# Four TensorE steps more for a quarter of the keys: merging runs of 128 to 256 in the matmul network of a sort on Trainium2

## The chip, the cores and the metric

The kernel runs on one core of a Trainium2 chip. The metric is the device time of one execution in microseconds (us), where less is better.

## What is computed

The input is 4 images of 64 x 64 tokens with 256 channels. The part that takes the time is the first layer. Each token is normalised over its channels, correlated with all 4,096 tokens of its image, and the 4,096 correlations are sorted; 256 evenly spaced ranks of the sorted row are added to the token:

```python
corr = jnp.einsum('bmf,bnf->bmn', x3, x3) / F
s = -jnp.sort(-corr, axis=-1)
ranks = jnp.round(jnp.linspace(1.0, M - 1, NB_POOLS)).astype(jnp.int32)
pooled = jnp.take(s, ranks, axis=-1)
```

After it comes a mixture of four experts with two layers each (256 to 512 to 256, GELU between), whose weights for a token come from a graph attention over 1,048,576 edges.

## The kernel before

`prepare` and `rank` (to about 4,290 us) normalise the tokens and work out where each edge goes. `pool_rows` is the sorting stage, to about 30,412 us. After it `segment_max`, `segment_sum`, `route` and `combine` do the attention and put the outputs together.

`pool_rows` works on 64 pairs of token tiles (2 x 128 tokens). A token's row of 4,096 keys lies in one partition, the two tiles being two halves `g` of the work. The sort has two parts.

**The front** sorts groups of 128 keys. TensorE and ScalarE do it on data that lie with the keys in the partitions. A comparison of keys a and z is written as a sum and a difference: TensorE multiplies by a matrix that gives a + z and a - z (`net`, built from `group_matrices`), ScalarE takes the absolute value (`ACT.Abs`, line 1189), and the next matrix makes (sum + |difference|) / 2 and (sum - |difference|) / 2 as part of its own sums. One such step is a tick. The 32 groups of a token's keys are handled in 4 rounds (`ROUNDS`) of 2 slots (`s`), each slot with 4 groups in two banks of PSUM. A round before the change has 29 ticks (`TICKS`):

- tick 0, the correlation: 8 matmuls of 256 columns a slot (line 992), copied by line 1186;
- 20 ticks whose comparisons stay within 64 wires (`BLOCK_TICKS`): four matmuls of 64 x 64 with 512 columns a slot, one in each quarter of the array (line 999). The prediction calls them tile ticks;
- 7 ticks of 128 x 128 matmuls, two a slot (line 1003): full ticks;
- the last, which turns the keys back so that tokens lie in the partitions (line 1008), copied by line 1195 into `fresh`.

A slot's next matmuls wait for ScalarE's copy of that slot (`fe_copied`), and ScalarE for them (`fe_ready`), so that one slot's matmuls run beside the other slot's copy. All operands are float32, and the profile counts two matmul records for each matmul.

**The merges** of the sorted runs, from 128 to 4,096, are VectorE's: 50 stages (`STAGES`), each with a pair (p, k), counted 0 to 49 in what follows. Stages 0 to 7 have p = 128, 8 to 16 p = 256, 17 to 26 p = 512, 27 to 37 p = 1,024, 38 to 49 p = 2,048. A stage does a maximum and a minimum (lines 1165 and 1166) for each half `g`. The last four stages (`SPARSE`, line 1141) compare only what the wanted ranks need. In a stage with k < p some keys at the ends of each run of 2p are not compared; ScalarE copies them to the other buffer (`carry`, line 1237): p keys of each 2p when k = p/2, half as many at each further stage.

**The order.** VectorE sorts pair i while TensorE and ScalarE do the front of pair i + 1 and the experts' layers (FFN) of pair i - 1. Nothing is scheduled by a planner. `ticks_of` spreads the ticks of a pair evenly over VectorE's first 48 stages; ScalarE's program (`period`) goes stage by stage: the copy of a stage for g = 0, its share of ticks, the copy for g = 1, more ticks. ScalarE's copy of stage s waits until VectorE has ended stage s - 1 (`sorted_`); VectorE's stage s + 1 waits for the copy of stage s (`carried`). VectorE's stage 0 waits for the whole front of its pair (line 1159). The FFN pieces on TensorE stand between ticks at fixed numbers: for expert e the first layer at ticks 31 + 20 e and the next, GELU on ScalarE at tick 34 + 20 e, the second layer at ticks 37 + 20 e and the next. `residual` follows VectorE's stage 4 and `normalise` stage 8. GpSimd scatters the edges all the while and is waited for by no one in this stage.

Of the kernel before, what the change touches and what calls it, by code (L numbers as in the profile page):

```python
# [16 lines left out]
F32 = mybir.dt.float32  # L17
BF16 = mybir.dt.bfloat16
I32 = mybir.dt.int32
ALU = mybir.AluOpType  # L20
# [3 lines left out]
P = 128  # L24
# [7 lines left out]
BANK = 512  # L32
# [38 lines left out]
C_ALL = C_LIFT + 1  # L71
# [7 lines left out]
def group_stages():  # L79

    out, p = [], 1
# [10 lines left out]
def group_pairs(p, k):  # L92
    out = []
    for at in range(0, WIRES, 2 * p):
        if k == 0:
            out += [(at + n, at + 2 * p - 1 - n) for n in range(p)]
        else:
            out += [(c + n, c + k + n) for c in range(at, at + 2 * p, 2 * k) for n in range(k)]
    return out


GROUP_STAGES = group_stages()
TICKS = len(GROUP_STAGES) + 1
BLOCK_TICKS = [t for t, (p, k) in enumerate(GROUP_STAGES) if t > 0 and 2 * p <= HALF]
assert len(BLOCK_TICKS) % 2 == 0


def group_matrices():

    out, wires = [], None
    for p, k in GROUP_STAGES:
        block = HALF if 2 * p <= HALF else WIRES
        rows = [(m // (block // 2) * block + m % (block // 2), pair) for m, pair in enumerate(group_pairs(p, k))]
        if wires is None:
            wires = np.eye(WIRES, dtype=np.float32)
        stage = np.zeros((WIRES, WIRES), np.float32)
        for r, (a, z) in rows:
            stage[:, r] = wires[:, a] + wires[:, z]  # L120
            stage[:, r + block // 2] = wires[:, a] - wires[:, z]
        out.append(stage)
        wires = np.zeros((WIRES, WIRES), np.float32)
        for r, (a, z) in rows:
            wires[r, a] = wires[r + block // 2, a] = wires[r, z] = 0.5
            wires[r + block // 2, z] = -0.5
    return out + [wires]


C_TOTAL = C_NET + TICKS * WIRES  # L130


def shape_constants():
# [14 lines left out]
    c[:, C_NET:] = np.concatenate(group_matrices(), 1)  # L148
# [20 lines left out]
N_FULL = N_STAGES - SPARSE  # L169

# [77 lines left out]
def build(nc, x, w_gat, att_src, att_dst, b_gat, ln_gamma, ln_beta, w1, b1, w2, b2, edges, consts, out):  # L248
# [35 lines left out]
    net = sb("net", [P, TICKS, WIRES], F32)  # L284
# [55 lines left out]
def prepare(nc, b):  # L340
# [50 lines left out]
    with nc.Block() as block:  # L391
        @block.sync
        def _(sp):

            sp.dma_start(b.cst[:], b.consts[:, 0:C_ALL]).then_inc(const_in, 16)
            sp.dma_start(b.net[:].rearrange("p t w -> p (t w)"), b.consts[:, C_NET:]).then_inc(const_in, 16)
# [1436 lines left out]
```

## Time and profile before

Three runs took 33,436.27 to 33,437.55 us, median 33,436.87. The profiled execution took 33,442.64 us, and the span of its profile is 33,441.0 us.

| engine | busy us | share of the span |
|---|---|---|
| TensorE, matmuls (PE) | 26,912.7 | 80% |
| TensorE, weight loads (PEld, beside PE) | 12,865.6 | 38% |
| VectorE (DVE) | 29,959.0 | 90% |
| ScalarE (ACT) | 20,929.2 | 63% |
| GpSimd (POOL) | 16,416.8 | 49% |

| group | count | busy us |
|---|---|---|
| tile ticks, matmul records, line 999 | 81,920 | 10,881.2 |
| full ticks, matmul records, line 1003 | 14,336 | 6,422.3 |
| copies with absolute value, line 1189 | 13,824 | 13,748.3 |
| maxima of the merges, line 1165 | 5,888 | 12,122.0 |
| minima of the merges, line 1166 | 5,888 | 12,114.5 |
| copies of kept keys, line 1237 | 5,632 | 3,338.5 |

Busy time of PE is modelled, so a busy PE is not PE at its peak. A duration is longer than the distance to the next start on the same engine, since the end of one instruction overlaps the beginning of the next; for sums, starts are compared. In a row of the timeline, square brackets give the idle time ahead of the instruction and what ended it. "issue" means that the engine waited for nothing that the profile shows.

### The profile page before, as it was taken

Reading aid. Unit: us, or ns where it says so; the run is one execution under the profiler, and the core shown is the slowest. Engines: PE = TensorE matmul, PEld = TensorE weight load, DVE = VectorE, ACT = ScalarE, POOL = GpSimd, SP = SyncE. Lnnn points to the kernel's source line nnn. Section 1 sums busy time; section 2 is a strip of 40 time slices with the busy share of each in tenths; the row PEclk is TensorE's granted clock in tenths of the full one; section 3 lists DMA queues with packets and bytes.
Section 4 is the critical chain, followed back from the end, with each engine's and each line's share of the span. In section 5 each row is a group of like instructions: output and inputs, shape, how many; then the busy total and the mean of one; then the engine's idle time right before and its main releaser. Section 6 shows DMA issues by size and latency. Waiting matters only on the chain. (4 is left out here: it accounts for less than half of the span.)

```text
span 33441.0 us, 482974 instructions
## 1 busy us (share of the span) xinstructions
PE 26912.7 (80%) x157939; PEld 12865.6 (38%) x158452; DVE 29959.0 (90%) x32518; ACT 20929.2 (63%) x31151; POOL 16416.8 (49%) x9076
## 2 busy tenths in 40 slices
PE   3888888888888888888888888888888888873464
PEld 3555533333333333333333333333333333332364
DVE  6888859999999999999999999999999999997744
ACT  2777766666667676667666666766766766760010
POOL 0000038888888888888888888883000000003520
PEclk8999999999999999999999999999999999996655
DMA  2000000000000000000000000000000000000103
GB/s 85 2 2 2 2 17 6 6 7 6 6 6 11 6 7 6 7 6 7 6 11 7 6 6 6 7 6 6 10 6 5 6 6 5 6 5 12 12 11 126
DMA packets 651133, 394.32 MB, mean 12 GB/s; under 512 B 424844, under 2 KB 604048, under 8 KB 646160
## 3 DMA queue, kind: packets, MB, share of 16 engines
q1 hardware_dynamic: 337746, 311.61, 3.0%
q0 software_dynamic: 290304, 22.40, 1.0%
q8 instruction: 1430, 23.43, 0.3%
q10 hardware_dynamic: 20288, 25.70, 0.2%
q14 instruction: 1365, 11.18, 0.1%
HBM read 196.68 MB, written 162.34 MB: 11 GB/s over the span
## 5 line engine op out<-in xcount | busy, mean ns | idle before, releaser
L1189 ACT ACTIVATE z<-psum 128x1024 f32<-128x1024 f32 x13824 | 13748.3, 1027 | 4795.4 <-PE psum L1003 2380.5
L1301 POOL DMA_INDIRECT sorted_d<-word_s,place_s x8192 | 15441.3, 1885 | 2646.8 <-issue 2476.9
L999 PE MATMUL psum<-z,net 64*64 64x512 f32 x81920 | 10881.2, 632 | 2974.8 <-ACT z L1189 2877.8
L1165 DVE TENSOR_TENSOR arena<-arena 128x2048 f32<-128x2048 f32 (+9 forms) x5888 | 12122.0, 2059 | 1216.7 <-ACT arena L1237 729.1
L1166 DVE TENSOR_TENSOR arena<-arena 128x2048 f32<-128x2048 f32 (+9 forms) x5888 | 12114.5, 2057 | 0.0
L1003 PE MATMUL psum<-z,net 128*128 128x512 f32 x14336 | 6422.3, 602 | 366.9 <-ACT z L1189 365.6
L999 PEld LDWEIGHTS psum<-z,net 64*64 64x64 f32 x81920 | 2567.8, 135 | 10337.6 <-issue 10323.0
L1452 POOL DMA_INDIRECT arena<-table_d,arena x752 | 901.6, 1199 | 8210.3 <-issue 7724.9
L1237 ACT ACTIVATE arena<-arena 128x2048 f32<-128x2048 f32 (+8 forms) x5632 | 3338.5, 594 | 1384.6 <-DVE arena L1166 1139.7
L1003 PEld LDWEIGHTS psum<-z,net 128*128 128x128 f32 x14336 | 2706.7, 192 | 3821.1 <-issue 2538.8
L823 ACT ACTIVATE arena<-cst,arena 128x128 bf16<-128x128 f32 x8320 | 2633.5, 389 | 608.4 <-PE psum L751 510.8
L1295 POOL DMA_DIRECT2D word_s<-words_d x64 | 37.4, 584 | 4802.1 <-issue 4664.9
L992 PE MATMUL psum<-rows,arena 128*128 128x256 f32 x8192 | 1836.3, 382 | 152.0 <-issue 120.2
L676 DVE TENSOR_SCALAR arena<-iota_bf,arena 128x256 bf16<-128x256 bf16 x8287 | 1791.7, 279 | 5.8 <-PE psum L751 5.7
L992 PEld LDWEIGHTS psum<-rows,arena 128*128 128x128 f32 x8192 | 1542.6, 191 | 379.3 <-issue 151.9
L712 DVE TENSOR_REDUCE arena<-psum 128x512 f32 x2048 | 1410.3, 689 | 289.6 <-PE psum L782 164.3
L1186 ACT ACTIVATE z<-psum,cst 128x1024 f32<-128x1024 f32 x512 | 570.1, 1113 | 1503.6 <-PE psum L992 1503.6
L1436 PE MATMUL psum<-cst,arena 128*128 128x128 f32 x3008 | 651.0, 407 | 972.2 <-DVE arena L1410 972.2
L1048 PE MATMUL psum<-arena,hid 128*128 128x256 f32 x4096 | 1144.5, 403 | 189.8 <-ACT hid L1221 189.8
L740 PE MATMUL psum<-arena,order_bf 128*128 128x128 bf16 x8320 | 851.4, 227 | 495.4 <-DVE arena L676 482.8
L1035 PE MATMUL psum<-tt,arena 128*128 128x256 f32 x4096 | 1131.1, 400 | 4.3 <-ACT tab L1213 4.3
L1141 DVE TENSOR_TENSOR arena<-arena 128x146 f32<-128x146 f32 (+16 forms) x3584 | 1037.5, 378 | 41.0 <-DVE arena L1141 24.1
(213 smaller groups left out, 16717.4 us busy)
## 6 DMA issues: line engine op xcount, KB each, us to landing
sorted_d<-word_s,place_s POOLq DMA_INDIRECT x8192
y_d<-ys SPq DMA_DIRECT2D x256, 256.0 KB
arena<-y_d SPq DMA_DIRECT2D x64, 1024.0 KB, 5.6
arena<-in_x SPq DMA_DIRECT2D x34, 512.0 KB, 5.1
x<-in_x SPq DMA_DIRECT2D x65, 256.0 KB
xnt_d<-arena SPq DMA_DIRECT2D x32, 512.0 KB, 3.1
hk_d<-arena SPq DMA_DIRECT2D x32, 512.0 KB, 4.3
arena<-hk_d SPq DMA_DIRECT2D x4, 4096.0 KB, 14.2
```

The lines of the kernel that those rows point to most:

```text
L676: last = nc.vector.tensor_scalar(hot_pair(slot, j), b.iota_bf[:], tile, None, ALU.is_equal)
L712: nc.vector.tensor_reduce(places[:, bass.ds(k * SUPER + g * 4, 4)], psum[:, g % 4, :].rearrange("p (q c) -> p q c", c=P), AX.X, ALU.max).t ...
L823: last = nc.scalar.activation(steps[:, j % RING, :], b.iota, ACT.Relu, bias=low_s[s][:, j:j + 1], scale=-1.0)
L992: last = nc.tensor.matmul(bank[:, n // 2, n % 2 * 2 * P:(n % 2 + 1) * 2 * P], b.xnt[:, c, key:key + WIRES], rows[:, c, :], start=(c == 0), ...
L999: last = nc.tensor.matmul(psum[n * HALF:(n + 1) * HALF, 2 * s + r, :], b.net[rr, t, rr], flat[rr, n * BANK:(n + 1) * BANK], start=True, st ...
L1003: last = nc.tensor.matmul(bank[:, n, :], b.net[:, t, :], flat[:, n * BANK:(n + 1) * BANK], start=True, stop=True)
L1048: nc.tensor.matmul(psum[:, 6 + g, 0:D], hid[:, m, g * P:(g + 1) * P], b.w2s[:, e, m, :], start=(m == 0), stop=False)
L1165: nc.vector.tensor_tensor(hi_out, hi_in, lo_in, ALU.max)
L1166: nc.vector.tensor_tensor(lo_out, hi_in, lo_in, ALU.min).then_inc(sorted_[g], 1)
L1189: last = nc.scalar.activation(flat, bank, ACT.Abs)
L1237: nc.scalar.activation(carried_over(half[s % 2][g], p, k), carried_over(half[(s - 1) % 2][g], p, k), ACT.Copy).then_inc(carried[g], 1)
L1301: pool.indirect_dma_start(out=b.sorted_d[:, :], out_offset=bass.IndirectOffsetOnAxis(ap=place_s[:, s, j:j + 1], axis=0), in_=word_s[:, s, ...
```

## The change

In the first of the four rounds the front now goes one level further. Its 1,024 keys leave it as 4 sorted runs of 256 instead of 8 of 128. To that end one of the two groups that are to be merged is sorted in the other order: half of the groups get their correlation with the sign changed (scale -1/D instead of 1/D, in two instructions of half the size), the step that makes both meet adds a bias of +2 or -2 (`C_MEET`), and the wires of a comparison then span 256 keys, of which TensorE sees 128 at a time.

VectorE's stages 0 to 7 and ScalarE's copies there leave out those 1,024 keys of each half (`LO`). Stage 8 reads them from `fresh` and the other 3,072 from where stage 7 left them, with two pairs of instructions for each half. ScalarE may therefore write `fresh` again only after stage 8 of the sort in progress (`FRESH_READ`).

The network of all rounds is laid out anew. Sorting 16 keys takes 9 layers instead of 10, so a round has 28 ticks instead of 29 (the correlation, 26 comparisons, the one out). The wires are split into halves by another of their bits at each level, so that comparisons stay within 64 wires of the array. Where the split changes, a new kind of tick stands, "swapped": four matmuls a slot of 64 rows x 128 columns with 512 columns streamed, two of them adding up in each bank (line 1113). The kinds of ticks:

| | correlation | tile | swapped | full | out | ticks |
|---|---|---|---|---|---|---|
| before, each of 4 rounds | 1 | 20 | 0 | 7 | 1 | 29 |
| after, round 0 | 1 | 29 | 2 | 3 | 1 | 36 |
| after, rounds 1 to 3 | 1 | 24 | 2 | 0 | 1 | 28 |

A pair has 120 ticks instead of 116, spread over the same 48 stages. The numbers at which FFN pieces stand are unchanged.

TensorE's program shows the new kinds. This is the first round of pair 2's front from its first tile tick on, up to the next round's correlation, before; names are the tensors written and read, and x is how many matmuls follow each other:

```order
L999 MATMUL psum<-z,net 64x512 x160
L1003 MATMUL psum<-z,net 128x512 x14
L1017 MATMUL psum<-cst,pooled 128x128 x4
L1003 MATMUL psum<-z,net 128x512 x12
L1025 MATMUL psum<-wtab,tt 128x24 x4
L1003 MATMUL psum<-z,net 128x512 x2
L1008 MATMUL psum<-net,z 128x128 x16
L992 MATMUL psum<-rows,arena 128x256 x16
```

And the same place after, up to the round's last full tick (line 1106 is a tile tick, 1113 a swapped one, 1117 a full one, 1099 the correlation):

```order
L1106 MATMUL psum<-z,net 64x512 x152
L1113 MATMUL psum<-z,net 128x512 x8
L1106 MATMUL psum<-z,net 64x512 x28
L1132 MATMUL psum<-cst,pooled 128x128 x4
L1106 MATMUL psum<-z,net 64x512 x4
L1117 MATMUL psum<-z,net 128x512 x4
L1106 MATMUL psum<-z,net 64x512 x8
L1117 MATMUL psum<-z,net 128x512 x2
L1140 MATMUL psum<-wtab,tt 128x24 x4
L1117 MATMUL psum<-z,net 128x512 x2
L1106 MATMUL psum<-z,net 64x512 x24
L1117 MATMUL psum<-z,net 128x512 x2
```

The block of seven full ticks is gone; single full and swapped ticks stand among tile ticks, and every FFN piece (here 1132 and 1140) keeps its tick number but has other neighbours.

VectorE's program around stages 7 and 8 in the loop, before:

```order
L1165 TENSOR_TENSOR arena<-arena 128x16x127
L1166 TENSOR_TENSOR arena<-arena 128x16x127
L1165 TENSOR_TENSOR arena<-arena 128x16x127
L1166 TENSOR_TENSOR arena<-arena 128x16x127
L1165 TENSOR_TENSOR arena<-arena 128x8x256
L1166 TENSOR_TENSOR arena<-arena 128x8x256
L1165 TENSOR_TENSOR arena<-arena 128x8x256
L1166 TENSOR_TENSOR arena<-arena 128x8x256
```

And after:

```order
L1287 TENSOR_TENSOR arena<-arena 128x12x127
L1288 TENSOR_TENSOR arena<-arena 128x12x127
L1287 TENSOR_TENSOR arena<-arena 128x12x127
L1288 TENSOR_TENSOR arena<-arena 128x12x127
L1287 TENSOR_TENSOR arena<-arena 128x2x256
L1288 TENSOR_TENSOR arena<-arena 128x2x256
L1287 TENSOR_TENSOR arena<-arena 128x6x256
L1288 TENSOR_TENSOR arena<-arena 128x6x256
L1287 TENSOR_TENSOR arena<-arena 128x2x256
L1288 TENSOR_TENSOR arena<-arena 128x2x256
L1287 TENSOR_TENSOR arena<-arena 128x6x256
L1288 TENSOR_TENSOR arena<-arena 128x6x256
```

Stage 7 runs over 12 runs instead of 16, and stage 8 is cut in two parts for each half. The diff, cut to its core:

```diff
+SORT16 = (((0, 5), (1, 4), (2, 12), (3, 13), (6, 7), (8, 9), (10, 15), (11, 14)),
...
+def layers():
+
+    out = [[(c + 15 - b, c + 15 - a) for c in range(0, WIRES, 16) for a, b in layer] for layer in SORT16]
+    p = 16
     while p < WIRES:
-        out.append((p, 0))
+        out.append([(c + n, c + 2 * p - 1 - n) for c in range(0, WIRES, 2 * p) for n in range(p)])
         k = p // 2
         while k >= 1:
-            out.append((p, k))
+            out.append(halving(WIRES, k))
             k //= 2
         p *= 2
...
+LAYERS = [[(side + a, side + z) for side in (0, WIRES) for a, z in layer] for layer in layers()]
+UP_TO_32 = len(LAYERS) - 7
+
+SORT_PLAN = ([("corr", LAYERS[0], by_64)] + [("tile", x, by_64) for x in LAYERS[1:UP_TO_32]]
+             + [("swapped", LAYERS[UP_TO_32], by_bit0)] + [("tile", x, by_bit0) for x in LAYERS[UP_TO_32 + 1:-2]])
+LAST_PLAN = [("tile", LAYERS[-2], by_bit0), ("swapped", LAYERS[-1], no_block)]
+MERGE_PLAN = ([("full", LAYERS[-2], by_bit3), ("tile", LAYERS[-1], by_bit3),
+               ("full", halving(256, 128), by_low)] + [("tile", halving(256, k), by_low) for k in (64, 32, 16)]
+              + [("full", halving(256, 8), by_side)] + [("tile", halving(256, k), by_side) for k in (4, 2)]
+              + [("swapped", halving(256, 1), no_block)])
+
...
+MERGED_ROUNDS = 1
+LO = MERGED_ROUNDS * SLOTS * UNIT_GROUPS * WIRES
+ROUNDS = M // WIRES // UNIT_GROUPS // SLOTS
+FRONT = [ticks_of_round(MERGE_PLAN, len(SORT_PLAN) + 1 + len(LAST_PLAN)) if j < MERGED_ROUNDS else
+         ticks_of_round(LAST_PLAN, len(SORT_PLAN) + 1) for j in range(ROUNDS)]
+TICK_OF = [(j, t) for j in range(ROUNDS) for t in range(len(FRONT[j]))]
+PER_PAIR = len(TICK_OF)
+LAST_FIRST = PER_PAIR - len(FRONT[-1]) + 1
...
+    c[:, C_MEET] = np.where(r % HALF < HALF // 2, 2.0, -2.0)
...
+    FRESH_READ = FIRST_MERGE + 1 if LO > 0 else 1
...
-                elif t in BLOCK_TICKS:
+                elif how == "tile":
                     for r in range(2):
                         rr = slice(r * HALF, (r + 1) * HALF)
                         for n in range(2):
-                            last = nc.tensor.matmul(psum[n * HALF:(n + 1) * HALF, 2 * s + r, :], b.net[rr, t, rr],
-                                                    flat[rr, n * BANK:(n + 1) * BANK], start=True, stop=True)
-                elif t < TICKS - 1:
+                            last = nc.tensor.matmul(psum[n * HALF:(n + 1) * HALF, 2 * s + r, :],
+                                                    b.net[rr, at:at + HALF], flat[rr, n * BANK:(n + 1) * BANK],
+                                                    start=True, stop=True)
+                elif how == "swapped":
+                    for r in range(2):
+                        for n in range(2):
+                            nn = slice(n * HALF, (n + 1) * HALF)
+                            last = nc.tensor.matmul(bank[:, n, :], b.net[nn, at + r * WIRES:at + (r + 1) * WIRES],
+                                                    flat[nn, r * BANK:(r + 1) * BANK], start=(r == 0), stop=(r == 1))
+                elif how == "full":
                     for n in range(2):
-                        last = nc.tensor.matmul(bank[:, n, :], b.net[:, t, :], flat[:, n * BANK:(n + 1) * BANK],
+                        last = nc.tensor.matmul(bank[:, n, :], b.net[:, at:at + WIRES], flat[:, n * BANK:(n + 1) * BANK],
                                                 start=True, stop=True)
                 else:
                     for g in range(2):
                         for n in range(UNIT_GROUPS):
-                            last = nc.tensor.matmul(bank[:, g, n * WIRES:(n + 1) * WIRES],
-                                                    z[s][:, n, g * P:(g + 1) * P], b.net[:, t, :],
+                            place = n % 2 * 2 + n // 2 if j < MERGED_ROUNDS else n
...
+            def sources(s, g):
+
+                last = half[(s - 1) % 2][g]
+                if s < FIRST_MERGE:
+                    return [(fresh[g] if s == 0 else last, LO, M)]
+                if s == FIRST_MERGE and LO > 0:
+                    return [(fresh[g], 0, LO), (last, LO, M)]
+                return [(last, 0, M)]
...
-                        nc.vector.tensor_tensor(hi_out, hi_in, lo_in, ALU.max)
-                        nc.vector.tensor_tensor(lo_out, hi_in, lo_in, ALU.min).then_inc(sorted_[g], 1)
+                        for source, from_, to in sources(s, g):
+                            hi_in, lo_in = compared(source[:, from_:to], p, k)
+                            hi_out, lo_out = compared(half[s % 2][g][:, from_:to], p, k)
+                            nc.vector.tensor_tensor(hi_out, hi_in, lo_in, ALU.max)
+                            last = nc.vector.tensor_tensor(lo_out, hi_in, lo_in, ALU.min)
+                        last.then_inc(sorted_[g], 1)
...
+                    if how == "corr" and j < MERGED_ROUNDS:
+                        for n in range(2):
+                            last = nc.scalar.activation(flat[:, n, :], bank[:, n, :], ACT.Abs,
+                                                        bias=b.cst[:, C_LIFT:C_LIFT + 1],
+                                                        scale=(1.0 - 2.0 * n) / D)
...
+                        if tick + 1 == len(FRONT[0]) and s == 0 and not (isinstance(i, int) and i == 0):
                             for g in range(2):
-                                act.wait_ge(sorted_[g], (i - 1) * N_FULL + 1)
+                                act.wait_ge(sorted_[g], (i - 1) * N_FULL + FRESH_READ)
...
+                    elif meet:
+                        last = nc.scalar.activation(flat, bank, ACT.Abs, bias=b.cst[:, C_MEET:C_MEET + 1])
+                    else:
+                        last = nc.scalar.activation(flat, bank, ACT.Abs)
...
-                nc.scalar.activation(carried_over(half[s % 2][g], p, k), carried_over(half[(s - 1) % 2][g], p, k),
-                                     ACT.Copy).then_inc(carried[g], 1)
+                first = LO if s < FIRST_MERGE else 0
+                nc.scalar.activation(carried_over(half[s % 2][g][:, first:M], p, k),
+                                     carried_over(half[(s - 1) % 2][g][:, first:M], p, k), ACT.Copy).then_inc(carried[g], 1)
```

## Rows read from the trace of the kernel before

**Rows 1.** Windows: length; busy us of PE, PEld, DVE, ACT, POOL; PE clock; DMA

```profile
4286.00:4664.00 378.00, 315.69 (x1815) 126.33 (x1813) 18.88 (x25) 235.06 (x240) 0.00 (x0) 0.95 0.10 36
13000.00:22000.00 9000.00, 7783.70 (x42853) 3289.98 (x42852) 8603.52 (x6049) 6280.78 (x7710) 7620.57 (x4143) 0.98 0.03 7
30412.00:33441.00 3029.00, 1473.35 (x6924) 1389.03 (x6924) 1735.15 (x3239) 169.47 (x406) 901.62 (x752) 0.57 0.18 44
```

**Rows 2.** Waits of VectorE, 10000 to 20000 us: total, times, longest

```profile
DVE arena L1165 <- ACT arena L1237: 289.7, 149, 5.1
DVE pooled L1141 <- ACT arena L1237: 70.5, 25, 3.5
DVE arena L1165 <- issue: 52.3, 25, 2.6
```

**Rows 3.** Timeline of VectorE: start us, us, engine, line, instruction, count [idle before]

```profile
15120.26 2.29 DVE L1165 TENSOR_TENSOR arena<-arena 128x2048 f32<-128x2048 f32 x1 [1.93 <-issue]
...
15129.07 1.22 DVE L1165 TENSOR_TENSOR arena<-arena 128x1024 f32<-128x1024 f32 x1
...
15133.62 1.75 DVE L1165 TENSOR_TENSOR arena<-arena 128x1536 f32<-128x1536 f32 x1
...
15331.04 2.29 DVE L1165 TENSOR_TENSOR arena<-arena 128x2040 f32<-128x2040 f32 x1 [5.14 <-ACT arena L1237]
...
20163.93 2.28 DVE L1165 TENSOR_TENSOR arena<-arena 128x2040 f32<-128x2040 f32 x1 [5.14 <-ACT arena L1237]
...
20298.86 2.16 DVE L1165 TENSOR_TENSOR arena<-arena 128x1920 f32<-128x1920 f32 x1 [4.01 <-ACT arena L1237]
```

**Rows 4.** Waits of ScalarE, 10000 to 20000 us

```profile
ACT arena L1237 <- DVE arena L1166: 311.0, 147, 4.3
```

**Rows 5.** Timeline of TensorE while no other work runs (first unit groups)

```profile
4378.31 24.30 PE L1003 MATMUL psum<-z,net 128*128 128x512 f32 x56
4402.44 3.73 PE L1008 MATMUL psum<-net,z 128*128 128x128 f32 x32
4406.01 7.07 PE L992 MATMUL psum<-rows,arena 128*128 128x256 f32 x32
...
4414.38 2.05 PE L999 MATMUL psum<-z,net 64*64 64x512 f32 x16 [0.28 <-ACT z L1186]
4416.70 1.62 PE L999 MATMUL psum<-z,net 64*64 64x512 f32 x12 [0.27 <-ACT z L1189]
```

**Rows 6.** Timeline of ScalarE, ticks with copies of kept keys

```profile
15129.07 1.93 ACT L1189 ACTIVATE z<-psum 128x1024 f32<-128x1024 f32 x2
...
15132.67 1.95 ACT L1189 ACTIVATE z<-psum 128x1024 f32<-128x1024 f32 x2
15134.48 1.09 ACT L1237 ACTIVATE arena<-arena 128x1024 f32<-128x1024 f32 x1
15135.43 1.97 ACT L1189 ACTIVATE z<-psum 128x1024 f32<-128x1024 f32 x2
```

**Rows 7.** Timeline of TensorE, FFN pieces between ticks

```profile
15230.00 1.09 PE L999 MATMUL psum<-z,net 64*64 64x512 f32 x8
15231.02 1.13 PE L1035 MATMUL psum<-tt,arena 128*128 128x256 f32 x4
15232.08 1.09 PE L999 MATMUL psum<-z,net 64*64 64x512 f32 x8
...
15250.03 1.13 PE L1048 MATMUL psum<-arena,hid 128*128 128x256 f32 x4
...
15258.58 1.95 PE L999 MATMUL psum<-z,net 64*64 64x512 f32 x16
...
15292.82 1.03 PE L1035 MATMUL psum<-tt,arena 128*128 128x256 f32 x4
15293.68 1.88 PE L1003 MATMUL psum<-z,net 128*128 128x512 f32 x4
```

**Rows 8.** The page's costliest groups: count | busy us, mean ns | idle before

```profile
L1003 PEld LDWEIGHTS psum<-z,net 128*128 128x128 f32 x14336 | 2706.7, 192 | 3821.1 <-issue 2538.8
```

More of the change, by code:

```diff
@@ L89, in group_stages @@
     return out
-def group_pairs(p, k):
-    out = []
-    for at in range(0, WIRES, 2 * p):
-        if k == 0:
-            out += [(at + n, at + 2 * p - 1 - n) for n in range(p)]
-        else:
[L98 to L127, printed above, removed]
@@ L130, with by_64, by_bit0, by_bit3 @@
-C_TOTAL = C_NET + TICKS * WIRES
+def by_64(w):
+    return w // 64 % 2
+def by_bit0(w):
+    return (w ^ w // 64) % 2
+def by_bit3(w):
+    return w // 8 % 2
+def by_low(w):
+    return w % 2
+def by_side(w):
+    return w // 128
+def no_block(w):
+    return 0
+def items_of(layer):
+    alone = set(range(2 * WIRES)) - {w for pair in layer for w in pair}
+    return [(0, a, z) for a, z in layer] + [(1, w, w) for w in sorted(alone)] + [(2, a, z) for a, z in layer]
+def in_rows(layer, blocks, at):
+    return sorted(m for m in items_of(layer) if all(f(m[1]) == v for f, v in zip(blocks, at)))
@@ new lines, in wire_from, with matrix @@
+def wire_from(layer, wire):
+    for a, z in layer:
+        if wire == a:
+            return {(0, a, z): 0.5, (2, a, z): 0.5}
+        if wire == z:
+            return {(0, a, z): 0.5, (2, a, z): -0.5}
+    return {(1, wire, wire): 1.0}
+def matrix(before, rows, item_list, turned):
+    m = np.zeros((len(rows), len(item_list)), np.float32)
+    index = {item: n for n, item in enumerate(rows)}
+    for n, (kind, a, z) in enumerate(item_list):
+        for wire, sign in ((a, 1.0),) if kind == 1 else ((a, 1.0), (z, 1.0 if kind == 0 else -1.0)):
+            for item, part in wire_from(before, wire).items() if before else {(1, wire, wire): 1.0}.items():
+                m[index[item], n] += sign * part * (-1.0 if wire >= WIRES and turned else 1.0)
+    return m
@@ new lines, with ticks_of_round @@
+SORT_NET, SORTED_16, INSIDE = plan_matrices(SORT_PLAN, None, None)
+LAST_NET = plan_matrices(LAST_PLAN, SORTED_16, INSIDE)[0]
+MERGE_NET = plan_matrices(MERGE_PLAN, SORTED_16, INSIDE)[0]
+WIRES_NET = matrix(LAYERS[-1], in_rows(LAYERS[-1], (no_block, by_side), (0, 0)), [(1, w, w) for w in range(WIRES)],
+                   False)
+NETS = SORT_NET + [WIRES_NET] + LAST_NET + MERGE_NET
+NET_AT = [sum(m.shape[1] for m in NETS[:n]) for n in range(len(NETS) + 1)]
+NET_COLS = NET_AT[-1]
+def ticks_of_round(plan, first):
+    wires = len(SORT_PLAN)
+    at = [NET_AT[n] for n in list(range(wires)) + list(range(first, first + len(plan)))]
+    out = [(how, a, layer == halving(2 * WIRES, WIRES)) for (how, layer, _), a in zip(SORT_PLAN + plan, at)]
+    return out + [("wires", NET_AT[wires], False)]
@@ L169 @@
 N_FULL = N_STAGES - SPARSE
+FIRST_MERGE = sum(p == WIRES for p, _ in STAGES)
 def compared(buf, p, k):
@@ L974, in _, with front @@
         def _(pe):
-            def front(i, j, t, s):
-                if j == 0 and t == 0 and s == 0:
+            def front(i, tick, s):
+                j, t = TICK_OF[tick]
+                how, at, _ = FRONT[j][t]
+                if tick == 0 and s == 0:
                     pe.wait_ge(hk_in, (i // PAIRS_OF_IMAGE + 1) * 16)
                     pe.wait_ge(rows_in, (i + 1) * 16)
-                before = j * TICKS + t
-                if not (isinstance(i, int) and i == 0 and before == 0):
-                    pe.wait_ge(fe_copied[s], i * PER_PAIR + before)
-                    if t in BLOCK_TICKS:
+                if not (isinstance(i, int) and i == 0 and tick == 0):
+                    pe.wait_ge(fe_copied[s], i * PER_PAIR + tick)
+                    if how in ("tile", "swapped"):
                         pe.sem_inc(b.settled[3], 1)
```

89 lines of the change are left out of this document (54 added, 35 removed), and 8 rows, old and new, of the table SORT16.

## The prediction, made before the kernel after was run

> **What bounds the kernel now.** I read the views from coarse to fine. First the windows: between 13,000 and 22,000 us VectorE is busy 95.6% of the time, TensorE 86%, ScalarE 70%, at a mean TensorE clock of 0.98 [rows 1]. That is the sorting stage, 64 pairs of token tiles from about 4,664 to 30,412 us, and the change touches nothing else but the 378 us ahead of it. Then the waits of VectorE: in 10,000 us it waits 289.7 + 70.5 us for ScalarE's copies (line 1237) and 52.3 us at the loop's turn [rows 2]. The timeline gives the length of a pair: the same wait of 5.14 us comes back after 12 pairs, (20163.93 - 15331.04) / 12 = 402.74 us [rows 3]. In 10,000 us there are thus 24.8 pairs, VectorE waits 16.6 us in each and has work of its own for 386. ScalarE in turn waits 311.0 / 24.8 = 12.5 us a pair for a full stage of VectorE [rows 4]. So VectorE sets the pace, with the TensorE-ScalarE chain close behind. Both must get shorter for a full gain.
>
> **What goes on VectorE.** A stage is four instructions, two for each half. Four of 2,048 elements take 15129.07 - 15120.26 = 8.81 us, four of 1,024 take 4.55 us [rows 3]; so an instruction costs 0.069 us + 1.04 ns an element, start to start. The eight stages of p = 128 hold 2048 + 1024 + 1536 + 1792 + 1920 + 1984 + 2016 + 2032 = 14,352 elements an instruction, and a quarter of them goes: 3,588 x 4 x 1.04 ns = 14.9 us. Stage 8 takes its keys from two places, which adds four instructions of 0.069 us: 0.3 us. Net 14.65 us a pair. The elements themselves stay at the same price, since only the outer count in the access pattern falls from 16 to 12.
>
> **What changes on TensorE and ScalarE.** A tick is one step of the small network for both slots. While no other work runs, the rows give: a tile tick (64x64) 2.31 us (4414.38 to 4416.70), a full tick 24.13 / 7 = 3.45, the tick that brings out the keys 3.6, the correlation 7.0 [rows 5]. Before, a round is one correlation, 20 tile ticks, 7 full ones and one out: 80.9 us. After, three rounds have 24 tile ticks, 2 of the new "swapped" kind and no full one: 66.1 us + 2 S. The first round has 29 tile ticks, 3 full, 2 swapped: 87.9 us + 2 S.
>
> S is in no row. Its slot has four matmuls of 64 rows x 128 columns; the two of a pair lie in different halves of the rows and write different banks. The lower bound is a full tick, 3.45 us, if the two run side by side. The upper bound is 6.9 if they don't, and somewhat more if each also pays a change of shape. The nearest row is the tile slot: four matmuls, in both halves of rows and of columns, take 1.02 us, where one full matmul takes 0.86 (two records of 0.431) [rows 5, 7]. So halves do run side by side, and I stay near the low end. Going from one shape to another costs 0.2 us: an FFN piece takes 1.06 us between tile slots (15231.02 to 15232.08) and 0.86 us in a full stretch (15292.82 to 15293.68) [rows 7]. A swapped tick has two such changes, so S = 3.45 + 0.35 = 3.8. By that, the four rounds go from 323.6 to 316.3 us. On the worst end (6.9) they become 341.
>
> The Trainium skill speaks against the change here. Its page TensorE: Matmul & The Clock Gate, section Part 3: Packing small matmuls, says that a weight load overlaps running matmuls only when its row group differs, and in a swapped slot the second pair's weights go into the rows that the first pair is using. By it S would be near 5. This case's rows say otherwise for one shape: 56 full matmul records in a row, all in the same rows and each with a load of 192 ns, take 0.431 us each, no more than their columns need [rows 5, 8]. I keep that result as the second rival.
>
> ScalarE has eight more slot passes of 0.9 us (1.81 us for two, 15132.67 to 15134.48 [rows 6]), 7.2 us. Its copies for p = 128 shrink by a quarter, about 1.6 us. The correlation of the first round is copied in two pieces, some 0.3 us under the longer matmuls. The new bias goes into a full tick, where ScalarE has time.
>
> **Whether the chain still keeps up.** I add up both engines stage by stage. ScalarE may start stage s's copy when VectorE has ended stage s-1, and VectorE's stage s+1 needs that copy. A tile tick costs 2.31, or 1.81 plus the copy if that is more: with a copy of 2,048 it takes 15132.67 - 15129.07 = 3.60, so the copy is 1.80; one of 1,024 is 0.95 [rows 6]. To it come the FFN pieces: 0.92 for each of 16 first-layer pieces, 1.24 for each of 16 second-layer ones. (15250.03 to 15258.58, with the slot after it 9.57 us for four slots and four pieces, less 4 x 1.16 [rows 7].) GELU adds about 1.5 us four times.
>
> For the kernel before, this sum gives waits of 1.6 and 5.0 us at stage 25 (the trace: 1.5 and 5.14), 3.5 us at stage 42 (4.01 or less) [rows 3], 4.7 at the pair's end, and 399.7 us a pair. So it misses 3 us of 402.74, and it finds the right places: each time the 7 full ticks, the one out and the next correlation put ScalarE behind.
>
> For the kernel after, with S = 3.8, stages 0 to 7 end at 49.1 us on VectorE (64.0 before) and ScalarE's ticks for them at 50.5 (61.3). ScalarE may be one stage late, so the early stages just fit. At stage 14 it stands at 95.7 against 100.3, at stage 25 at 185.0 against 188.2, where before it was 198.5 against 211.7. The waits left are 0.9 at stage 17, 1.7 at 31, 1.2 at 41, some tenths elsewhere and 3.9 at the pair's end, which stays since a swapped tick and the one out stand there as full ones did. The pair takes 378.7 us, 21.0 less: 14.65 of work, 6.3 of waits. With S = 3.45 it is 376.6, with S = 5 386.4.
>
> **Sum.** 62 pairs run with both neighbours: 62 x 21.0 = 1,302 us. The first and the last have no such waits and give 14.65 each: 29. The network ahead of the first pair gives 323.6 - 316.3 = 7. Together 1,338 us. The profiled execution took 33,442.64 us (span 33,441.0), 5.8 over the median of 33,436.87, so I subtract from either alike: 32,105 by the profile, 32,100 by the median. This is 4.0% faster.
>
> **Rivals.**
> 1. The waits don't fall or new ones come, since a swapped tick is dearer (S about 5: four exposed loads of 192 ns in a slot, 3.45 + 2 x 0.77). The pair takes 386.4, 13.3 less; 62 x 13.3 + 29 - 2 = 852 us, so 32,585. For it: the early stages have only some us to spare. Against it: the 56 records above.
> 2. The two halves of a swapped tick run one after the other (S = 6.9). The pair takes 399.7, as before: what VectorE saves it waits at stages 17 to 42. Only the ends differ, 29 saved and 18 lost: 33,425, no change. Against it: the tile slot [rows 7].
> 3. Slower: as rival 2, and each of the four matmuls also pays the 0.2 us of a change of shape, 4 x 1.06 a slot, S = 8.5. The sum gives 410.9 a pair; 62 x 11.2 + 30 - 29 = 695 us more, so 34,130. It decides from S = 6.9 on. Only the place, the eight swapped ticks of each pair, could do it.
> 4. All waits for ScalarE vanish but the pair's end: 402.74 - 14.65 - 12 = 376.1, that is 26.65 less a pair; 62 x 26.65 + 29 + 7 = 1,688 us, so 31,755. The sum finds small waits instead, so this is only the floor.
>
> **Chances.** The forecast has 0.72 (with the part toward the floor), rival 1 has 0.18, rival 2 0.04, rival 3 0.05, and 0.01 is left. The range goes from 31,930 (S = 3.45 and a few more us of waits gone) to 32,620, just beyond rival 1. A change of 0.2% is 67 us, about what a measurement of this kernel can tell from none. Faster is the forecast, rival 1 and the rest, 0.91; same is rival 2, 0.04; slower is rival 3, 0.05.
>
> **What would show it.** In the new profile VectorE's stages of p = 128 show 1,536 elements and 1.67 us from start to start instead of 2,048 and 2.20; its busy time falls by 64 x 15 = 950 us. A swapped tick shows eight matmul records a slot and ScalarE's slots there 1.7 to 2.0 us apart; 2.5 would be rival 1, 3.4 rival 2. The pair's length, read from a wait that comes back, is 380 to 383 us, and VectorE's waits for line 1237's successor fall from 14.5 to about 9 us a pair. The forecast is wrong if those waits grow, above all at stages 2 to 8, or if TensorE's clock in the sorting stage falls below 0.98, since a stretch of tile ticks keeps TensorE less busy than one of full ticks.

## The result, and the profile after

The kernel after takes 32,594.52 us (median of 4 runs, 32,555.5 to 32,615.38), the one before 33,436.57 (4 runs, 33,435.37 to 33,437.55). The ratio is 0.9747, 95% interval 0.973 to 0.9764: 2.5% faster. The forecast was 32,105 us with a range of 31,930 to 32,620. So the sign and the range held, but only 842 of the 1,338 us came. The time is that of rival 1 (32,585), and the question is whether that is more than chance. The end of the range had been put just beyond that rival, so that the time lies inside it says little for the forecast.

First the windows of after, with the columns of [rows 1]: a stretch where GpSimd scatters, and one behind it.

```profile
13000.00:22000.00 9000.00, 7709.95 (x50208) 3051.51 (x50204) 8543.43 (x6287) 6616.95 (x8175) 7562.29 (x4298) 0.98 0.03 7
24000.00:28000.00 4000.00, 3452.07 (x22631) 1367.15 (x22624) 3837.35 (x2799) 2976.99 (x3683) 0.00 (x0) 0.99 0.02 6
```

VectorE's share hardly moved: 94.9% in the first window (95.6% before). In the second it is 95.9%. GpSimd's busy time is 0 there: the last of its indirect DMAs for the sorted words is issued at 22,037 us, when some 30% of the stage is still to come.

From one residual addition of VectorE (line 1215) to the next, the 63 distances sum to 24,494.4 us (25,323.4 before): 829 of the 842 us come from the pairs. Before, a pair took 402.8 us everywhere but at the ends. After, the first 44 took 390.9 on the mean, between 385 and 396, and the 18 behind them 386.2, most of them 385.5 and some 388 to 390. Two misses thus stand apart, one in every pair and one only beside the scatter. They can be seen in the waits of VectorE (total, times, longest; as [rows 2]), first from 10,000 to 20,000 us, then from 24,000 to 28,000:

```profile
DVE arena L1287 <- ACT arena L1370: 251.6, 256, 3.1
DVE arena L1287 <- issue: 114.1, 57, 3.5
DVE pooled L1254 <- ACT arena L1370: 96.1, 21, 5.2
DVE pooled L1254 <- issue: 17.8, 5, 3.6
...
DVE arena L1287 <- ACT arena L1370: 88.6, 92, 2.6
DVE pooled L1254 <- ACT arena L1370: 42.9, 10, 5.1
DVE arena L1287 <- issue: 21.2, 10, 2.3
```

A late pair waits (88.6 + 42.9 + 21.2) / (4000 / 386.2) = 14.7 us. Its own work on VectorE is 386.2 - 14.7 = 371.5 us. The first window gives 479.6 / 25.6 = 18.7 us a pair. Before it was 16.6. So the waits of VectorE fell by 1.9 us in a late pair, where 6.3 had been forecast, and beside the scatter they grew by 2.1. The sum had forecast 7.7 us of waits in a pair of 378.7.

Where a late pair waits, the timeline of VectorE shows (start us, us, ..., idle before). The line numbers are those of after: 1254 is the sparse stages and 1287 the full ones.

```profile
26105.47 1.98 DVE L1254 TENSOR_TENSOR pooled<-arena 128x20 f32<-128x20 f32 x15 [4.02 <-ACT arena L1370]
...
26109.81 1.76 DVE L1287 TENSOR_TENSOR arena<-arena 128x1536 f32<-128x1536 f32 x1 [2.28 <-issue]
26111.49 1.75 DVE L1288 TENSOR_TENSOR arena<-arena 128x1536 f32<-128x1536 f32 x1
...
26126.32 1.56 DVE L1287 TENSOR_TENSOR arena<-arena 128x1344 f32<-128x1344 f32 x1 [1.20 <-ACT arena L1370]
...
26235.97 2.29 DVE L1287 TENSOR_TENSOR arena<-arena 128x2048 f32<-128x2048 f32 x1 [2.57 <-ACT arena L1370]
...
26346.62 2.16 DVE L1287 TENSOR_TENSOR arena<-arena 128x1920 f32<-128x1920 f32 x1 [1.90 <-ACT arena L1370]
```

The stages of p = 128 have 1,536 elements and start 26111.49 - 26109.81 = 1.68 us apart, as forecast. The 5.14 us of stage 25 and the 4.01 of stage 42 [rows 3] are gone. What is left: 1.20 at stage 3, 2.57 at stage 17, 1.90 at stage 31, and 4.02 + 2.28 at the pair's end, with 0.6 at stage 27 and 0.9 at stage 41. That end is the largest item. It looks like this on ScalarE, and then on TensorE:

```profile
26084.82 1.92 ACT L1328 ACTIVATE z<-psum 128x1024 f32<-128x1024 f32 x2
26093.51 0.21 ACT L1370 ACTIVATE arena<-arena 128x8 f32<-128x8 f32 x1 [6.77 <-DVE arena L1254]
26093.62 1.92 ACT L1328 ACTIVATE z<-psum 128x1024 f32<-128x1024 f32 x2
```

```profile
26086.22 1.95 PE L1106 MATMUL psum<-z,net 64*64 64x512 f32 x16 [2.35 <-ACT z L1328]
26094.77 5.59 PE L1113 MATMUL psum<-z,net 64*128 64x512 f32 x16 [6.61 <-ACT z L1328]
26100.29 3.84 PE L1123 MATMUL psum<-net,z 128*128 128x128 f32 x32
```

ScalarE's copy for stage 47 waits 6.77 us until VectorE has done sparse stage 46. The tick behind that copy waits with it, TensorE stands idle 6.61 us, and then the round's last two ticks (swapped and out) still have to run. The copy that VectorE needs for its last stage is queued behind them. In addition TensorE's granted clock falls from 1.00 to 0.50, the lower of its two levels (2.4 and 1.2 GHz). These are stretches of 2 us, with the busy time of PE, the granted clock and the DMA's share and rate:

```profile
26090.00:26092.00 2.00, 0.00 (x0) 0.95 0.00 0
26092.00:26094.00 2.00, 0.00 (x0) 0.50 0.00 0
...
26096.00:26098.00 2.00, 2.00 (x6) 0.50 0.03 8
26098.00:26100.00 2.00, 2.00 (x10) 0.85 0.00 0
```

The engine stood idle from 26,088.2 us on; the clock is low from about 26,092 to 26,098.6, and the swapped tick takes 5.52 us (26094.77 to 26100.29) where another of the same pair, at the full clock, takes 3.63 (26070.10 to 26073.73). So it goes in all pairs: the idle time there is 4.9 to 6.7 us, and the tick takes 5.0 to 6.7.

### The profile page after: what moved, and what is told of

Read it like the earlier page. It is cut to its first block and busy times, and to the rows that moved or that the text cites. A ratio compares the mean times of both kernels' runs of the same rounds, so it can differ in the third digit from the quotient of the medians.

```text
span 32598.3 us, 522374 instructions
## 1 busy us (share of the span) xinstructions
PE 26112.8 (80%) x175347; PEld 11892.7 (36%) x175348; DVE 29043.6 (89%) x32774; ACT 21326.7 (65%) x31791; POOL 15496.0 (48%) x9076
## 5 line engine op out<-in xcount | busy, mean ns | idle before, releaser
L1328 ACT ACTIVATE z<-psum 128x1024 f32<-128x1024 f32 x14208 | 14119.6, 1026 | 3874.4 <-PE psum L1106 2531.0
L1433 POOL DMA_INDIRECT sorted_d<-word_s,place_s x8192 | 14521.6, 1773 | 2646.6 <-issue 2476.6
L1106 PE MATMUL psum<-z,net 64*64 64x512 f32 x103424 | 13524.6, 616 | 2673.1 <-ACT z L1328 2440.0
L1287 DVE TENSOR_TENSOR arena<-arena 128x1536 f32<-128x1536 f32 (+17 forms) x6016 | 11641.9, 1935 | 1194.4 <-ACT arena L1370 598.6
L1288 DVE TENSOR_TENSOR arena<-arena 128x1536 f32<-128x1536 f32 (+17 forms) x6016 | 11633.6, 1934 | 0.0
L1106 PEld LDWEIGHTS psum<-z,net 64*64 64x64 f32 x103424 | 3114.0, 132 | 11895.5 <-issue 11880.4
L1370 ACT ACTIVATE arena<-arena 128x2048 f32<-128x2048 f32 (+15 forms) x5632 | 3221.9, 573 | 987.6 <-DVE arena L1288 543.4
L1113 PE MATMUL psum<-z,net 64*128 64x512 f32 x8192 | 2052.7, 637 | 557.0 <-ACT z L1328 548.9
L1113 PEld LDWEIGHTS psum<-z,net 64*128 64x128 f32 x8192 | 955.6, 200 | 1701.2 <-issue 1660.4
L1316 ACT ACTIVATE z<-psum,cst 128x1024 f32<-128x1024 f32 x384 | 427.8, 1114 | 1036.8 <-PE psum L1099 1036.8
L1163 PEld LDWEIGHTS psum<-arena,hid 128*128 128x128 f32 x4096 | 700.7, 190 | 1043.7 <-issue 808.3
```

What stands on the lines that cost most here:

```text
L1106: last = nc.tensor.matmul(psum[n * HALF:(n + 1) * HALF, 2 * s + r, :], b.net[rr, at:at + HALF], flat[rr, n * BANK:(n + 1) * BANK], start=T ...
L1113: last = nc.tensor.matmul(bank[:, n, :], b.net[nn, at + r * WIRES:at + (r + 1) * WIRES], flat[nn, r * BANK:(r + 1) * BANK], start=(r == 0) ...
L1163: nc.tensor.matmul(psum[:, 6 + g, 0:D], hid[:, m, g * P:(g + 1) * P], b.w2s[:, e, m, :], start=(m == 0), stop=False)
L1287: nc.vector.tensor_tensor(hi_out, hi_in, lo_in, ALU.max)
L1288: last = nc.vector.tensor_tensor(lo_out, hi_in, lo_in, ALU.min)
L1328: last = nc.scalar.activation(flat, bank, ACT.Abs)
```

## The experiments

All times are medians and are compared with the kernel before on the same chip (33,446.7 to 33,447.1 us); a ratio is to that kernel. The 32,594.5 us of the kernel after were measured beside 33,436.6 us of the kernel before, so a difference between an experiment and the kernel after can be off by some 10 us.

**1. After, without the scatter.** In the loop of GpSimd the waits and the indirect DMAs are left out, so the sorted words are not written:

```diff
-                    for j in range(SCAT):
-                        pool.indirect_dma_start(
-                            out=b.sorted_d[:, :], ...
```

> The kernel after, with GpSimd's 8,192 indirect DMAs of the sorting stage left out (the edges are not scattered, so the attention and the experts' weights are not the reference's). In the kernel after a pair takes 391 us until about 21,600 us, while these DMAs run, and 385.5 us later; in the kernel before it takes 402.75 all the time. Theory A: TensorE's program, which now has 1,012 matmuls a pair instead of 880, nearly all in short tile ticks, runs out of instructions when the scatter's DMAs slow their fetching; then without the scatter every pair takes 385.5 us, TensorE's 'issue' waits ahead of tile ticks (110 us in all) go, and the time is about 43 x 5.8 = 250 us lower than the kernel after's 32,594: 32,345. Rival B: the later pairs are faster for a reason of their own place or data; then the time stays within 30 us of 32,594.

Measured: 32,464.22 us, ratio 0.9707 (0.9687 to 0.9726). The pairs took 386.2 us on the mean, early ones and late ones alike. This is the pairs' gain that was expected of the scatter theory, but the time fell by 130 us only. Experiment 2 says where the rest is. What the scatter does to a pair, after's trace shows. TensorE in a pair beside the scatter:

```profile
10143.81 1.09 PE L1106 MATMUL psum<-z,net 64*64 64x512 f32 x8 [0.30 <-issue]
10145.06 1.09 PE L1106 MATMUL psum<-z,net 64*64 64x512 f32 x8 [0.16 <-ACT z L1328]
10147.91 1.82 PE L1106 MATMUL psum<-z,net 64*64 64x512 f32 x8 [1.76 <-issue]
```

and VectorE there:

```profile
10145.67 1.56 DVE L1287 TENSOR_TENSOR arena<-arena 128x1344 f32<-128x1344 f32 x1 [1.34 <-ACT arena L1370]
10150.78 1.56 DVE L1287 TENSOR_TENSOR arena<-arena 128x1344 f32<-128x1344 f32 x1 [2.08 <-issue]
10154.87 1.66 DVE L1287 TENSOR_TENSOR arena<-arena 128x1440 f32<-128x1440 f32 x1 [1.06 <-ACT arena L1370]
```

TensorE stops for 1.76 us with nothing to wait for that the profile shows. VectorE then waits 1.34 + 2.08 + 1.06 = 4.48 us at stages 3 and 4, where the late pair waits 1.20. These stops ahead of tile ticks add up to 24 to 29 us in each 5,000 us of the kernel after, from 5,000 to 20,000 us. Two thirds of the 126 are under 0.5 us, and the longest is 3.2. They are absent behind 22,100 us and absent without the scatter. Two things stay open. The stops are only some 1.9 us a pair, where the pair gets 4.7 us longer. And of VectorE's additional waits some 2.4 us are at stages 2 to 4, near which most of the stops lie, but 1.5 us are at stages 15 and 16, with hardly a stop there. That a stop makes VectorE wait is read from pairs like this one; that the scatter costs the pairs this much is shown by the experiment.

**2. Before, without the scatter** (the same edit).

> The kernel before with the same 8,192 DMAs left out (output as in e1). Theory A (instructions): the kernel before shows hardly any such waits (12 us in all), so it stays at 33,437 within 20 us. Rival C: the scatter slows ScalarE's or VectorE's accesses to memory in any kernel; then this kernel too becomes faster, by 100 us or more.

Measured: 33,521.99 us, ratio 1.0023 (1.0012 to 1.0033), and pairs of 402.4 to 403.2 us as with it. So the scatter costs the pairs of before nothing. But the kernel gets slower, by 75 us, and that is in the gather behind the sort. VectorE's products there (their idle time last), with the scatter and without it:

```profile
L1410 DVE TENSOR_TENSOR arena<-arena 128x2048 f32<-128x2048 f32 x188 | 430.9, 2292 | 300.6 <-DMA arena<-table_d,arena 149.4 <-PE psum L1436 117.6 <-issue 33.6
```

```profile
L1400 DVE TENSOR_TENSOR arena<-arena 128x2048 f32<-128x2048 f32 x188 | 430.9, 2292 | 385.1 <-DMA arena<-table_d,arena 385.1
```

VectorE's idle time there is 385.1 - 300.6 = 84.5 us longer. All of it now ends with one of the gather's DMAs, where these ended 149.4 us of it before and TensorE most of the rest. The gather now takes its places from words that nobody wrote; that this is what slows its DMAs is argued and not tested. The side effect belongs to experiment 1 too, where the idle time is 385.5 us (299.4 in the kernel after). In the pairs experiment 1 saved 24,494 - 24,285 = 209 us, or 4.7 us in each of 44.

**3. The new network alone.**

```diff
-MERGED_ROUNDS = 1
+MERGED_ROUNDS = 0
```

> The kernel after with no round merged (MERGED_ROUNDS = 0): the new network with 28 ticks a round in all four rounds, VectorE's stages 0 to 7 whole again. Theory: the lighter network alone removes VectorE's waits for ScalarE at stages 25 and 42; the stage sum gives 388.7 us a pair where it gave 399.9 for the kernel before, so about 391.7; 62 x 11 = 680 us less by that, and some 200 of it lost again to instruction stalls while the scatter runs: 32,900 to 33,000. Rival: the gain of the change is all VectorE's shorter stages; then this kernel takes 33,437 within 70 us. Second rival: the merge brings nothing and the network all; then it takes 32,600.

Measured: 32,774.22 us, ratio 0.98 (0.9783 to 0.9816), pairs of 392 to 393 us throughout. The expectation was too high. The network with more tile ticks and swapped ones brings 672 us, and merging on top only 180. Here the scatter costs the pairs nothing. TensorE's issue waits at tile ticks are 15.5 us in 10,000, none over 0.8 us (49.0 and 3.2 in the kernel after), and ScalarE has slack, since it waits 692 us for VectorE's full stages in those 10,000. Which of the two spares the pairs is not separated. VectorE waits at the pair's end alone:

```profile
DVE pooled L1254 <- ACT arena L1370: 123.2, 26, 4.9
DVE arena L1287 <- issue: 56.5, 26, 2.5
```

**4. After, with its 120 ticks ending at step 46** instead of 47. Nothing is added or removed; the last ticks stand ahead of the copy for stage 47.

```diff
-        at = [min(PER_PAIR * n // FRONT_STEPS, PER_PAIR) for n in (step, step + 1)]
+        at = [PER_PAIR * n // FRONT_STEPS if n < FRONT_STEPS - 1 else PER_PAIR for n in (step, step + 1)]
```

> The kernel after, with the three ticks of step 47 (the last swapped one, the one before it and the one that brings out the keys) moved into step 46, so that they no longer wait for VectorE's stage 46. In the kernel after ScalarE waits up to 6.8 us for that stage, TensorE idles, its clock falls (0.56 granted there) and the next swapped tick takes 5.15 us instead of 3.7; VectorE then waits 4.0 and 2.3 us at the pair's end. Theory: that wait at the end goes down to about 2.3 us, by the stage sum 3.7 us a pair and a bit more since the clock stays up: 62 x 4 = 250 us less, 32,345. Rival: ScalarE only gets later in step 46, VectorE waits at stage 47 for the copy instead and the time stays within 60 us of 32,594.

Measured: 32,176.11 us, ratio 0.9619 (0.9603 to 0.9635), 418 us under the kernel after, where 250 were expected. The pairs took some 379 us behind the scatter and 384.1 beside it. TensorE at the pair's end:

```profile
26090.15 1.95 PE L1106 MATMUL psum<-z,net 64*64 64x512 f32 x16 [0.56 <-ACT z L1328]
26092.46 3.70 PE L1113 MATMUL psum<-z,net 64*128 64x512 f32 x16 [0.37 <-ACT z L1328]
26096.10 3.84 PE L1123 MATMUL psum<-net,z 128*128 128x128 f32 x32
```

and VectorE:

```profile
26107.49 1.99 DVE L1254 TENSOR_TENSOR pooled<-arena 128x20 f32<-128x20 f32 x15 [0.22 <-DVE arena L1254]
```

No idle time of 6 us, a swapped tick of 3.64 us, a granted clock of 1.00 throughout, and no wait at the last sparse stage. Some 7 us a pair are more than the 4.02 that stood there; the wait at stage 3 went with it and that at stage 17 shrank (2.57 to 1.56), since the next round starts earlier.

**5. After, with its ticks dealt by a table.** The stage sum of the prediction, put through a search over the ticks of each step, names this one (step 47 gets no tick, so experiment 4 is in it):

```diff
+    SHARE = (3, 2, 1, 2, 4, 3, 5, 2, 2, 2, 3, 1, 4, 2, 1, 2, 2, 2, 2, 2, 3, 4, 3, 3,
+             2, 3, 4, 1, 2, 2, 3, 2, 3, 3, 2, 3, 3, 2, 1, 2, 3, 4, 1, 3, 5, 3, 3)
-        at = [min(PER_PAIR * n // FRONT_STEPS, PER_PAIR) for n in (step, step + 1)]
+        at = [sum(SHARE[:n]) for n in (step, step + 1)]
```

> The changed kernel with its 120 ticks dealt to the 47 steps by a table (1 to 5 ticks a step) in place of the even division, and none at step 47. The stage sum gives 372.1 us a pair for it, against 377.9 for the changed kernel and 374.2 for the version whose ticks end at step 46. Theory (the stage sum is right where no ScalarE copy waits for a sparse stage, as the version ending at step 46 showed with 378.9 us a pair): 2 us a pair under that version after the scatter's end, so 376 to 378 us a pair and 31,950 to 32,080 us in all, with VectorE's waits at stages 31 and 41 gone. Rival (the sum's waits are finer than its stages are known, so a table fitted to it gains nothing): 32,130 to 32,230 us, and new waits of 1 to 2 us at stages where the sum has none.

Measured: 31,729.51 us, ratio 0.9486 (0.9471 to 0.9502). It beats both kernels, by 5.1% and 2.7%. The pairs took 375 to 376 us, beside the scatter as behind it, so the time is 220 us under the lower end of what was expected. Waits of VectorE, 10,000 to 20,000 us (1290 and 1373 are lines 1287 and 1370 of after):

```profile
DVE arena L1290 <- ACT arena L1373: 53.0, 35, 2.3
DVE arena L1290 <- issue: 47.8, 25, 2.0
```

That is 3.8 us a pair instead of 18.7. With the same matmuls in the same order and with the scatter running, TensorE's stops have shrunk too:

```profile
PE psum L1109 <- issue: 13.0, 50, 0.3
```

0.3 us is the longest (3.2 in the kernel after). So dense tile ticks beside a scatter don't make the stops by themselves.

**6. The new network alone, ticks ending at step 46** (the edits of 3 and 4).

> The new network without the merging (MERGED_ROUNDS = 0, 32,774 us), and its 112 ticks ending at step 46 instead of 47. Stage sum: 386.8 us a pair against 388.7, measured 392.6 for the latter. Theory (the wait at a pair's end belongs to the ticks of step 47, whatever the merging): the sparse stages' wait goes here too, 2 to 4 us a pair, so 32,520 to 32,640 us; the merging is then worth 350 to 460 us where it seemed worth 180. Rival (only the merging's longer chain of ticks makes the wait at the end, since ScalarE has slack without it): under 0.5 us a pair, 32,740 to 32,780 us, and the merging is worth 560 to 600 us.

Measured: 32,488.98 us, ratio 0.9714 (0.9698 to 0.973), pairs of 387.9 us: 285 us less, more than the theory's 2 to 4 us a pair. The wait at the pair's end is not a matter of merging. Against experiment 4 the merging is worth 313 us.

**7. Before, ticks ending at step 46** (the edit of 4, 116 ticks).

> The kernel before, with its 116 ticks ending at step 46 instead of 47. Stage sum: 399.2 us a pair against 399.9 (measured 402.7). Theory (the wait at the pair's end is small there, and the rest of its waits stand at stages 25 and 42, where the ending changes nothing): 0.5 to 1.5 us a pair, 33,350 to 33,410 us. Rival (TensorE's idle time and lower clock in the sparse stages cost this kernel as much as the changed one, 6.5 us a pair): 33,030 us, and the gain of the version ending at step 46 has little to do with the change.

Measured: 33,436.1 us, ratio 0.9995 (0.9986 to 1.0005). No change, less than the 0.5 to 1.5 us a pair expected, and the rival's 33,030 is far off. The waits moved: the last sparse stage's 70.5 us [rows 2] went, and others took their place, in 10,000 us and then in the timeline:

```profile
DVE arena L1165 <- ACT arena L1237: 306.0, 148, 5.1
DVE arena L1141 <- ACT arena L1237: 53.6, 25, 2.2
...
15107.47 2.94 DVE L1141 TENSOR_TENSOR arena<-arena 128x56 f32<-128x56 f32 x16 [2.17 <-ACT arena L1237]
...
15222.30 2.23 DVE L1165 TENSOR_TENSOR arena<-arena 128x1984 f32<-128x1984 f32 x1 [1.20 <-ACT arena L1237]
```

The stage ahead of the last sparse one now waits 2.17 us for its copy, so the next round starts only some 0.8 us earlier. That is lost again at stage 13, long before the wait of 5.14 us at stage 25. There the wait is 1.20 us; in the kernel before it is 0.41:

```profile
15226.97 2.23 DVE L1165 TENSOR_TENSOR arena<-arena 128x1984 f32<-128x1984 f32 x1 [0.41 <-ACT arena L1237]
```

In the three kernels tried, moving the end was worth something only with the new network (experiments 4 and 6).

**8. Before, with a table of its own.**

```diff
+    SHARE = (4, 2, 3, 2, 1, 5, 3, 4, 0, 2, 2, 2, 2, 3, 3, 5, 2, 1, 3, 2, 2, 2, 2, 2,
+             2, 5, 2, 3, 2, 2, 3, 2, 2, 2, 2, 3, 2, 5, 0, 2, 2, 3, 2, 2, 2, 4, 3)
```

> The kernel before, with its 116 ticks dealt to the 47 steps by a table of its own (0 to 5 ticks a step) in place of the even division. It asks what the change is worth when both kernels have their ticks where the sorting stages want them. The stage sum gives 386.8 us a pair, with no wait of VectorE left, against 399.9 with the even division (measured 402.7). Theory (the waits at stages 25 and 42 come of the division alone): 388 to 392 us a pair, 32,480 to 32,760 us, so that the change is worth 750 to 1,000 us beside the changed kernel with its own table (31,730 us). Rival (TensorE and ScalarE are themselves too slow here: the sum has 10 us of slack a pair on them, and 0.2 us more a tick would use it up and bring 12 us of waits back): 396 to 402 us a pair, 33,000 to 33,400 us, and the change is worth 1,270 us or more.

Measured: 33,084.9 us, ratio 0.989 (0.9874 to 0.9907), pairs of 396 to 398.5 us: in the rival's range. Part of it is a wait that my sum had not got:

```profile
PE psum L1020 <- DVE pooled L1122: 234.1, 25, 9.7
```

This table puts the tick with the LayerNorm's transpose at the start of step 9, and TensorE waits 9.4 us a pair there for the rows that VectorE normalises behind stage 8. So whether the old network has the slack that the sum gives it stays open. As run, the changed kernel is 33,084.9 - 31,729.5 = 1,355 us faster when both have a table, and 842 when neither has.

**9. The changed kernel with its table, without the scatter** (the edits of 5 and 1).

> The changed kernel with its ticks dealt by the table, and GpSimd's 8,192 indirect DMAs of the sorting stage left out (the sorted words are then not written). In the changed kernel, pairs took 391 us with them and 385.5 after them; under the table, 375.4 in both parts of the run. Theory (the table's order keeps TensorE's late instructions off the path, so the scatter costs it nothing): the pairs stay at 375.0 to 375.5 us, and the time is that of the table plus what leaving the scatter out adds to the gather behind the sort (about 85 us, as in the kernel before): 31,790 to 31,830 us. Rival (the scatter still slows every pair, by other means than waits that show): 1 us a pair or more, so 31,760 us or less.

Measured: 31,806.95 us, ratio 0.9509 (0.9493 to 0.9525), 77 us more than experiment 5. The gather's idle time is 80 us longer (303.5 to 383.8), and the pairs gained 3 us in all. Under the table, the scatter costs the pairs nothing.

## Why the prediction was off

*VectorE's work: right.* 14.65 us a pair less was forecast. 402.8 - 16.6 = 386.2 us of own work before and 371.5 after differ by 14.7. The page gives 29,043.6 us busy, 915 less (64 x 15 = 950 was forecast).

*The price of a swapped tick: right, near the low end.* Where the clock is full it takes what a full tick between tile ticks takes in the kernel after (3.63 us):

```profile
15499.69 3.70 PE L1113 MATMUL psum<-z,net 64*128 64x512 f32 x16 [0.42 <-ACT z L1328]
15503.33 3.84 PE L1123 MATMUL psum<-net,z 128*128 128x128 f32 x32
```

(the kernel of experiment 3.) 15503.33 - 15499.69 = 3.64 us, against 3.8 taken; in the kernel after it is 3.63 at the full clock. So rivals 1 to 3, which need 5, 6.9 and 8.5, are refuted. Rival 1's time came out by luck, for its mechanism did not: one of the eight swapped ticks of a pair does take 5 us and more, but for the clock and not for its loads. The Trainium skill's rule (TensorE: Matmul & The Clock Gate, section Part 3: Packing small matmuls), by which this tick's second loads could not overlap, does not agree with these 3.64 us.

*The waits: wrong.* This is the step "the waits left are 0.9 at stage 17, 1.7 at 31, 1.2 at 41 [...] and 3.9 at the pair's end". Its places were right, but the end and stage 17 were priced too low, and the wait at stage 3 was not in it.
- In every pair, 4.02 + 2.28 us were left at the end instead of 3.9, 2.57 at stage 17 instead of 0.9, and 1.20 at stage 3 instead of none. The late pairs came out 402.8 - 386.2 = 16.6 us shorter than before instead of 21.0. The prediction said that the end "stays since a swapped tick and the one out stand there as full ones did", and priced them with TensorE at full clock. In the trace the swapped tick there takes 5.52 us, behind 6.61 us of idle time, and most of it at a clock of 0.50. Experiment 4 moves the end and takes away the wait, the idle time and the 1.9 us of slower tick at once. How much of the 418 us each of them has is not separated. 4.4 us x 62 pairs = 273 us.
- Beside the scatter, 390.9 - 386.2 = 4.7 us came on top in each of 44 pairs, 207 us. Experiment 1 shows that it takes the scatter (209 us less in the pairs, the stops of TensorE gone); that it comes through the stops is argued from the timelines. The rival, that the pair's place in the program makes it slower, falls with that. The prediction had no term for it: the kernel before shows neither the stops (0.6 us in 10,000) nor a cost of the scatter (experiment 2). Its remark that "the early stages just fit" was the warning, and its sign of being wrong, growing waits at stages 2 to 8, came true there at stages 2 to 4.

273 + 207 = 480 of the 495 us. The rest is at the ends of the stage, for which 29 + 7 = 36 us were forecast: up to the first residual addition came 9.8 us (5,084.8 to 5,075.0), in the last distance 6.0, and behind it 4.

All waits for the copies of kept keys come to 13.6 us a pair beside the scatter and 12.7 behind it, where the prediction had about 9 (14.5 before). TensorE's mean clock in the sorting stage did not fall below 0.98.

What makes TensorE stop is not settled. It takes the scatter (1). Beside it the stops at tile ticks, in 10,000 us, are 49.0 us in the kernel after and 48.8 in experiment 4, but 13.0 under the table (5, none over 0.3 us), 15.5 in the network alone (3, none over 0.8) and 3.3 in experiment 6 (none over 0.4). So it also takes how the ticks stand between the stages; I have no run that says what in their position matters.

## What to carry to other kernels

When two engines are brought near to balance, price what is left at the turn of the loop with the idle time that stands ahead of it, and don't let work for the next round queue behind a wait for the slow last stages of this one. Then deal the work anew: against a table the even division cost the kernel before 1.1%, and the changed kernel 2.7%. A stage sum that is 3 us a pair off was good enough here to search for that division; where a wait was missing from it (experiment 8), the pairs came out some 10 us longer than the sum.

## What the hardware showed unexpectedly

- Matmuls of 64 rows x 128 columns in the two halves of the rows, each into a bank of its own, run side by side, and so do the two behind them that add into the same banks: 16 records in 3.64 us, 0.455 a pair, where a record of a full matmul takes 0.431 [rows 5].
- TensorE at a granted clock of 1.00 idled 6.6 us; within that time the clock went to 0.50, and it was back at 1.00 some 7 us later. In an earlier pair the same tick took 5.08 us (15579.19 to 15584.27) behind 6.06 us of idle time. It takes 3.64 where nothing idles.
- TensorE stops of up to 3.2 us ahead of tile ticks with nothing to wait for that the profile shows, seen in the kernel after only while GpSimd issues indirect DMAs: 24 to 29 us in 5,000 us, none behind the scatter, and none over 0.3 us under another division of the same ticks.
- A scatter that is left out can slow a gather elsewhere: VectorE stood idle for 385.1 us at the gather instead of 300.6, and all of that ended with one of its DMAs, instead of 149.4 us.
